# The context in two transfers, and a new order of W_audio's and W_text's first work on TensorE

## The chip, the cores and the metric

One core of a Trainium2 chip runs the kernel. The time is device microseconds (us) of one execution; lower is better. The engines are TensorE (PE; its weight loads are listed apart as PEld), VectorE (DVE), ScalarE (ACT), GpSimd (POOL) and SyncE (SP, which here only issues transfers; SPq and ACTq are the queues of issues). Each engine works through its own instructions in order and waits on semaphores for the others.

## What is computed

A cross attention: 4 batches of 2048 rows of x (512 wide) attend to 4 batches of 77 context rows (384 wide).

```python
text_p = einsum('bld,dh->blh', x, W_text) + b_text          # 512 -> 512
audio_p = einsum('bsd,dh->bsh', ctx, W_audio) + b_audio     # 384 -> 512
Q = layer_norm(text_p, g1, beta1)
K = layer_norm(audio_p, g2, beta2)
alpha = softmax(einsum('blh,bsh->bls', Q, K) / sqrt(512))
hyper = einsum('bls,bsh->blh', alpha, audio_p)
hyper = einsum('blh,hk->blk', hyper, W_out) + b_out
out = layer_norm(hyper + x, g_out, beta_out)
```

## The kernel before

The kernel does not form Q. In a setup it turns the weights and the context into per-batch matrices, among them the Gram matrix of the centred W_text, from which the variance of a row of `text_p` follows, and the score weights W_text x K. The steady part then takes x in 32 steps of 256 rows: TensorE transposes x and multiplies it with these matrices, ScalarE and VectorE split each operand in a high and a low part, and the rest of the layer norms and the softmax follows. The steady part is the same after the change. The change lies in the first third of the setup.

Every engine's program is written out by hand, and its order is the order of the work. The names that matter:

- SyncE (L315 to L325) issues the loads: the context `cx` (77 partitions, 4 batches, 384 columns; `ctx_loaded`), then blocks of 128 rows of W_audio (`load_audio(0..2)`) and of W_text (`load_text(0..3)`), then W_out. The next thing it issues are the loads of x, after `linear(1)` on VectorE.
- TensorE begins with ten warm-up products (`keep_busy`, L1190). Then come twelve transposes of the context (L1214, four for each block k of 128 columns, a batch each), which ScalarE copies to `cxT` (L576, in order of k). `audio_product(j, k)` (L1202) multiplies block j of W_audio with block j of the context into bank k; each takes two passes of 308 columns. It waits for `cxT_ready` of j + 1. The last one for bank k, j = 2, releases `audio(k)` on ScalarE (L564, two copies: `vT` and `vT_hi`).
- The vectors (g1, b_audio and others) are transposed (L1219) and copied by VectorE (L850, `vec_ready`).
- VectorE centres W_text: `centre_even(k)` itself (L834 to L836), `centre_odd` (L841) with a row sum that ScalarE makes (`text_sum`, L558, behind the three copies to `cxT` in ScalarE's order). `text_transposes(j)` (L1195) waits for block j to be centred; when the fourth block is through, ScalarE copies the high part (`wtT_hi`, L593, behind `audio(0)` in its order) and VectorE makes the low part (`text_lo(k)`, L871).
- VectorE also makes `gram_kept` and `gram_left` (L859 to L863), from which GpSimd makes `root` (L430); `root_cols` (L878) follows after the fourth `text_lo`. It sums and centres `b_text` (L866, L867, L879), and makes the low part of the projected context (`keys_lo(k)`, L892).
- TensorE's `gram(k)` (L1239) waits in its first round for `text_lo(h)`. After `gram(0)`, the transposes of the root (L1250) and the first half of `gram(1)` comes the mean over the projected context (L1260). It waits for all four `keys_lo` (`vT_lo_ready`). Behind it, in TensorE's order: the rest of `gram`, the values (L1284) and the key scales (L1294), with which VectorE goes on (L955).

The order on TensorE around the change, before:

```python
pe.wait_ge(ctx_loaded, 16)
for k in range(KA):
    ...                                  # four transposes, cxT_psum
for k in range(KH):
    audio_product(0, k)
...                                      # the transpose of the vectors
for k in range(KH):
    audio_product(1, k)
audio_product(2, 0)
...
text_transposes(0); text_transposes(1); text_transposes(2); text_transposes(3)
audio_product(2, 1); audio_product(2, 2); audio_product(2, 3)
```

Of the kernel before, what the change touches and what calls it, by code (L numbers as in the profile page):

```python
# [25 lines left out]
ALU = mybir.AluOpType  # L26
ACT = mybir.ActivationFunctionType
AX_X = mybir.AxisListType.X

P = 128  # L30
# [3 lines left out]
def cross_attention(nc, x, ctx, w_text, b_text, w_audio, b_audio, w_out, b_out,  # L34
                    g1, beta1, g2, beta2, g_out, beta_out, out):
    B, L, D = x.shape
    _, S, DA = ctx.shape
    H = w_text.shape[1]
    KD, KA, KH = D // P, DA // P, H // P
# [24 lines left out]
    with ExitStack() as stack:  # L64
        f32 = lambda ap: ap.bitcast(F32)

        def sb(name, shape, dt=F32):
            return stack.enter_context(nc.sbuf_tensor(name, shape, dt))

        def sem(name):  # L70
            return stack.enter_context(nc.semaphore(name))
# [14 lines left out]
        wtT_hi, wtT_lo = wtT[:, 0], wtT[:, 1]  # L86
# [37 lines left out]
        bt_rows = sb("bt_rows", [P, H])  # L124
# [12 lines left out]
        sums = sb("sums", [P, 16])  # L137
# [24 lines left out]
        cx = values[:, 0:B * DA].rearrange("p (b d) -> p b d", b=B)[0:S]  # L162
# [24 lines left out]
        wt_loaded = [sem(f"wt_loaded{k}") for k in range(KD)]  # L187
        wa_loaded = [sem(f"wa_loaded{j}") for j in range(KA)]
        wo_loaded = [sem(f"wo_loaded{n}") for n in range(2)]
        ctx_loaded, vec_loaded = sem("ctx_loaded"), sem("vec_loaded")  # L190
        bt_loaded, bo_loaded = sem("bt_loaded"), sem("bo_loaded")
        gs_loaded, t_copied = sem("gs_loaded"), sem("t_copied")
        mean_r_ready = sem("mean_r_ready")
# [6 lines left out]
        wtT_hi_ready, wtT_lo_ready, lin_ready = sem("wtT_hi_ready"), sem("wtT_lo_ready"), sem("lin_ready")  # L200
# [22 lines left out]
        W_BANK = (psT[:], B_BANK[0], psD[:], psO[:])  # L223
# [81 lines left out]
        def _(sp):  # L305
# [3 lines left out]
            def load_text(k):  # L309
                sp.dma_start(wt[:, k, :], wt_rows[:, k, :]).then_inc(wt_loaded[k], 16)  # L310

            def load_audio(j):
                sp.dma_start(wa[:, j, :], wa_rows[:, j, :]).then_inc(wa_loaded[j], 16)

            sp.dma_start(cx, ctx.rearrange("b s d -> s b d")).then_inc(ctx_loaded, 16)  # L315
            load_audio(0)
            load_text(0)
            load_audio(1)
            load_text(1)
            load_text(2)  # L320
            load_audio(2)
            load_text(3)
            wo_rows = w_out.rearrange("(k p) h -> p k h", p=P)
            for n in range(2):
                sp.dma_start(wo[:, 2 * n:2 * n + 2, :], wo_rows[:, 2 * n:2 * n + 2, :]).then_inc(wo_loaded[n], 16)  # L325
# [496 lines left out]
        def _(dve):  # L822
            own = [0]

            def link(ins):

                own[0] += 1
                ins.then_inc(dve_own, 1)
                dve.wait_ge(dve_own, own[0])
# [13 lines left out]
            def gram_dot(k):  # L843
                dve.wait_ge(wc_ready, k + 1)
                nc.vector.tensor_tensor_reduce(out=waste_dve[:, k, 0:H], in0=wt[:, k, :], in1=wt[:, k, :], scale=1.0, scalar=0.0,
                                               op0=ALU.mult, op1=ALU.add, accum_out=gram_diag[:, k:k + 1]).then_inc(gram_dot_ready, 1)
# [7 lines left out]
            gram_dot(2)  # L854
            gram_dot(3)

            dve.wait_ge(gram_sq_ready, 2)
            dve.wait_ge(gram_dot_ready, 2)
            nc.vector.tensor_scalar(gram_kept[:], gram_diag[:], KEPT, None, ALU.mult).then_inc(kept_ready, 1)  # L859
# [2 lines left out]
            dve.wait_ge(left_ready, 1)  # L862
            nc.vector.tensor_scalar(gram_left[:], gram_left[:], 1e-30, None, ALU.max).then_inc(left_ready, 1)  # L863

            dve.wait_ge(bt_loaded, 16)
            link(nc.vector.reduce_sum(sums[:, 4:5], bt_rows[:], axis=AX_X))  # L866
            link(nc.vector.tensor_scalar(sums[:, 5:6], sums[:, 4:5], -1.0 / H, None, ALU.mult))  # L867

            def text_lo(k):
                dve.wait_ge(wtT_hi_ready, k + 1)  # L870
                nc.vector.tensor_tensor(wtT_lo[:, k, :], W_BANK[k], f32(wtT_hi[:, k, :]), ALU.subtract).then_inc(wtT_lo_ready, 1)  # L871

            text_lo(0)
            text_lo(1)
            text_lo(2)
            text_lo(3)
            dve.wait_ge(root_ready, 1)
            nc.vector.tensor_copy(root_cols[:], root[:]).then_inc(root_cols_ready, 1)  # L878
            nc.vector.tensor_scalar(bt_rows[:], bt_rows[:], sums[:, 5:6], None, ALU.add).then_inc(bc_ready, 1)  # L879

            def t_lo(k):
# [300 lines left out]
        def _(pe):  # L1182
# [9 lines left out]
            def text_transposes(j):  # L1192
                pe.wait_ge(wc_ready, j + 1)
                for k in range(KH):
                    last = nc.tensor.transpose(W_BANK[k][:, j * P:(j + 1) * P], wt[:, j, k * P:(k + 1) * P], ident[:])  # L1195
                    if j == KD - 1:
                        last.then_inc(wtT_psum, 1)

            def audio_product(j, k):
                pe.wait_ge(wa_loaded[j], 16)  # L1200
                pe.wait_ge(cxT_ready, j + 1)
                last = nc.tensor.matmul(V_BANK[k][:, 0:BS], wa[:, j, k * P:(k + 1) * P], cxT[:, j, :],  # L1202
                                        start=(j == 0), stop=(j == KA - 1))
                if j == KA - 1:
                    last.then_inc(vT_psum, 1)
# [2 lines left out]
            pe.wait_ge(ones_ready, 1)  # L1208
            keep_busy(10, psE)
            pe.wait_ge(ident_ready, 1)  # L1210
            pe.wait_ge(ctx_loaded, 16)
            for k in range(KA):
                for b in range(B):
                    last = nc.tensor.transpose(CTX_BANK[k][:, b * S:(b + 1) * S], cx[:, b, k * P:(k + 1) * P], ident[0:S, 0:S])  # L1214
                last.then_inc(cxT_psum, 1)
            for k in range(KH):
                audio_product(0, k)
            pe.wait_ge(vec_loaded, 16 * len(VECS))
            nc.tensor.transpose(VEC_BANK[:, 0:len(VECS) * KH], vec_rows[:], ident[0:len(VECS) * KH, 0:len(VECS) * KH]).then_inc(vec_psum, 1)  # L1219
            for k in range(KH):  # L1220
                audio_product(1, k)
            audio_product(2, 0)
            pe.wait_ge(vec_ready, 1)
            pe.wait_ge(cxT_ready, KA)
            text_transposes(0)
            text_transposes(1)
            text_transposes(2)
            text_transposes(3)
            audio_product(2, 1)
# [284 lines left out]
```

## Time and profile before

| what | us |
|---|---|
| median of 3 runs (lowest, highest) | 264.65 (264.42, 264.94) |
| the profiled execution | 264.86 |
| its span, first to last instruction | 263.1 |
| TensorE busy in it | 251.4 (96%) |
| VectorE busy | 231.6 (88%) |
| ScalarE busy | 217.5 (83%) |
| GpSimd busy | 203.2 (77%) |

A share of busy time is an average over stages. The rows below give a start, a duration and what was waited for; with them one can follow which engine is last at a given point. Matmuls are pipelined, so the listed duration of one is longer than the time until the next can start; starts of successive instructions tell the pace.

### The profile page before, as it was taken

What the parts mean: (1) busy time and instruction counts of PE and PEld (TensorE: products, weight loads), DVE (VectorE), ACT (ScalarE), POOL (GpSimd) and SP (SyncE); (2) the same over time, 40 slices, a digit from 0 to 9 for tenths busy, and PEclk for the clock granted to TensorE, in tenths of its full rate; (3) what the DMA queues carried; (4) which work ended last, traced back from release to release, by engine and by line L of the source; (5) the groups of instructions that cost most, each with busy time, mean ns of one, the idle gap of its engine ahead of it and who ended that gap; (6) DMA issues with size and microseconds to landing.
All of it is one profiled execution on the core that took longest, in us unless ns stands there. A gap on an engine that the chain in (4) does not pass through costs nothing.

```text
span 263.1 us, 6007 instructions
## 1 busy us (share of the span) xinstructions
PE 251.4 (96%) x1671; PEld 234.4 (89%) x1671; DVE 231.6 (88%) x712; ACT 217.5 (83%) x575; POOL 203.2 (77%) x213
## 2 busy tenths in 40 slices
PE   8999999999999999999999999999999999999860
PEld 8789888989999999999999999999999999998730
DVE  0797799789999999999999999999999999999884
ACT  3696385246999999999999999999999999999970
POOL 8139450021399999999999999999999999999694
PEclk9999999999999999999999999999999999999997
DMA  6901769544345444454554445455444454553036
GB/s 196 357 2 40 183 216 392 166 120 151 105 148 163 171 166 165 168 167 166 167 166 159 159 161 159 161 159 159 161 159 166 168 166 172 168 173 148 0 161 239
DMA packets 19489, 43.26 MB, mean 164 GB/s; under 512 B 2082, under 2 KB 2414, under 8 KB 19466
## 3 DMA queue, kind: packets, MB, share of 16 engines
q1 hardware_dynamic: 18842, 41.96, 47.2%
q10 hardware_dynamic: 624, 1.06, 1.6%
q14 instruction: 17, 0.14, 0.2%
q8 instruction: 6, 0.10, 0.2%
HBM read 21.19 MB, written 16.78 MB: 144 GB/s over the span
## 4 chain that ended last, share of the span: by engine, by line
PE 79%; SPq 6%; DVE 5%; POOL 4%; issue 2%; ACT 1%; DMA 1%; POOLq 0%; DVEq 0%; ACTq 0%
PE psY L1407 26%; PE psY L1391 12%; PE psT L1320 10%; PE psO L1427 10%; SPq L344 6%; PE psY L1386 4%; PE psE L1370 3%; PE psE L1371 2%; PE psY L1202 2%; PE psE L1190 2%; POOL zs L525 1%; DMA xs<-in_x_dram 1%; PE psT L1284 1%; PE psT L1239 1%; POOL rstd L500 1%
## 5 line engine op out<-in xcount | busy, mean ns | idle before, releaser
L1407 PE MATMUL psY<-proj,x_hi 128*128 128x336 f32 x512 | 102.5, 322 | 0.0
L1407 PEld LDWEIGHTS psY<-proj,x_hi 128*128 128x128 f32 x512 | 84.1, 189 | 5.5
L475 POOL TENSOR_TENSOR zs<-zs,gain 128x512 f32<-128x512 f32 x55 | 71.2, 1294 | 3.8 <-ACT zs L696 3.8
L481 POOL TENSOR_TENSOR zs<-zs,shift 128x512 f32<-128x512 f32 x54 | 68.5, 1291 | 0.0
L487 POOL TENSOR_TENSOR rstd<-stat_eps,neg_half 128x4 f32<-128x4 f32 x30 | 30.5, 1017 | 33.1 <-DVE stat_eps L1044 33.1
L1391 PE MATMUL psY<-proj,x_lo 128*128 128x336 f32 (+1 forms) x256 | 54.2, 313 | 0.0
L1032 DVE CUSTOM_DVE_ANT_0 waste_dve<-psY,xs,sums 128x515 bf16<-128x515 f32 x64 | 48.4, 756 | 2.3
L1052 DVE SCALAR_TENSOR_TENSOR hid<-psO,inv_sum,xs 128x512 f32<-128x512 f32 x60 | 44.8, 747 | 3.2 <-PE psO L1427 0.6
L696 ACT ACTIVATE zs<-hid,shift,rstd 128x512 f32<-128x512 f32 x58 | 47.1, 813 | 0.0
L654 ACT ACTIVATE x_hi<-psT 128x512 fp32r<-128x512 f32 x64 | 38.1, 596 | 8.8 <-PE psT L1320 6.9
L685 ACT ACTIVATE waste_act<-hid,xs 128x512 bf16<-128x512 f32 x60 | 43.1, 718 | 1.4 <-DVE hid L1052 1.3
L907 DVE TENSOR_TENSOR x_lo<-psT,x_hi 128x512 fp32r<-128x512 f32 x64 | 43.7, 683 | 0.4 <-ACT x_hi L654 0.2
L1391 PEld LDWEIGHTS psY<-proj,x_lo 128*128 128x128 f32 x256 | 40.3, 189 | 0.0
L1320 PE MATMUL psT<-ident,xs 128*128 128x128 f32 x256 | 39.7, 278 | 0.1
L1320 PEld LDWEIGHTS psT<-ident,xs 128*128 128x128 f32 x256 | 28.1, 141 | 1.9 <-DMA xs<-in_x_dram 0.3
L1427 PE MATMUL psO<-wo_hi,parts_t 128*128 128x512 f32 x60 | 26.9, 448 | 0.2 <-ACT parts_t L727 0.2
L1386 PE MATMUL psY<-proj,x_lo 128*128 128x128 f32 (+1 forms) x128 | 26.8, 251 | 0.0
L713 ACT ACTIVATE psD<-logits,neg_max 128x77 f32<-128x77 f32 x62 | 19.8, 319 | 7.7 <-DVE neg_max L1067 7.7
L1427 PE MATMUL psO<-wo_lo,parts_t 103*128 103x512 f32 x60 | 23.9, 398 | 0.0
L1386 PEld LDWEIGHTS psY<-proj,x_lo 128*128 128x128 f32 x128 | 23.1, 188 | 0.0
L727 ACT ACTIVATE parts_t<-psE 128x512 fp32r<-128x512 f32 x31 | 18.6, 599 | 2.7 <-PE psE L1371 1.8
L1370 PE MATMUL psE<-ident,parts 128*128 128x128 f32 x62 | 15.9, 284 | 1.3 <-DVE parts L1077 1.3
(272 smaller groups left out, 430.8 us busy)
## 6 DMA issues: line engine op xcount, KB each, us to landing
xs<-in_x_dram SPq DMA_DIRECT2D x64, 256.0 KB, 3.0
out_dram<-zs SPq DMA_DIRECT2D x29, 512.0 KB, 3.9
proj<-proj SPq DMA_DIRECT2D x4, 768.0 KB, 6.9
out_dram<-zs SPq DMA_DIRECT2D x6, 256.0 KB, 2.2
xs<-in_L_xattn_W_text_dram SPq DMA_DIRECT2D x4, 256.0 KB, 5.4
xs<-in_L_xattn_W_out_dram SPq DMA_DIRECT2D x2, 512.0 KB, 7.4
wa<-in_L_xattn_W_audio_dram SPq DMA_DIRECT2D x3, 256.0 KB, 5.1
zs<-in_ctx_dram SPq DMA_DIRECT2D x1, 462.0 KB
```

The source lines that it names most:

```text
L475: nc.gpsimd.tensor_tensor(zs[:, q, t, :], zs[:, q, t, :], gain[:], ALU.mult).then_inc(zg_ready, 1)
L481: nc.gpsimd.tensor_tensor(zs[:, q, t, :], zs[:, q, t, :], shift[:], ALU.add).then_inc(out_ready, 1)
L685: nc.scalar.activation(waste_act[:, t, :], hid[:, (b - 3) % 2, t, :], ACT.Square, bias=sc[:, q, t, NX:NX + 1], accum_out=stat[:, (b + 1) % ...
L696: nc.scalar.activation(zs[:, q, t, :], hid[:, q % 2, t, :], ACT.Identity, bias=shift2[:, q, t:t + 1], scale=rstd[:, q, T + t:T + t + 1]).t ...
L907: nc.vector.tensor_tensor(x_lo[:, b % 2, t, :], psT[:], f32(x_hi[:, b % 2, t, :]), ALU.subtract).then_inc(x_lo_ready, 1)
L1032: nc.vector.tensor_tensor_reduce(out=waste_dve[:, t, 0:QUAD_W], in0=psY[:, t, QUAD_AT:QUAD_AT + QUAD_W], in1=xs_rows[:, q, t, X_AT - 1:X_A ...
L1052: nc.vector.scalar_tensor_tensor(hid[:, (b - 3) % 2, t, :], psO[:], inv_sum[:, q, t:t + 1], xs[:, q, t, :], ALU.mult, ALU.add).then_inc(hi ...
L1320: last = nc.tensor.transpose(psT[:, k * P:(k + 1) * P], xs[:, b, t, k * P:(k + 1) * P], ident[:])
L1386: return nc.tensor.matmul(psY[:, t, B_AT + SW + k * P:512], x_lo[:, par, t, k * P:(k + 1) * P], proj[:, q, k, SW + k * P:HALF], start=Fals ...
L1391: return nc.tensor.matmul(psY[:, t, 512 + skip:512 + HALF], x_lo[:, par, t, k * P:(k + 1) * P], proj[:, q, k, HALF + skip:ROW_W], start=Fa ...
L1407: nc.tensor.matmul(psY[:, t, to:to + HALF], x_hi[:, par, t, k * P:(k + 1) * P], proj[:, q, k, right * HALF:(right + 1) * HALF], start=(k = ...
L1427: last = nc.tensor.matmul(psO[:], parts_t[0:rows, (b - lag) % 2, t, n, :], v[0:rows, q, :], start=(n == 0), stop=(n == 1))
```

## The change

It touches four places. (1) The context comes in two transfers: its first 128 columns, then W_audio's first block, then the context's other 256 columns; each has a semaphore of its own. W_text's fourth block is loaded before W_audio's third. (2) On TensorE the four products of W_audio's first block stand right behind the first four context transposes, and the other eight transposes behind those products. (3) The first product of W_audio's third block moves from before W_text's transposes to between the second and the third of its four blocks. (4) On VectorE `text_lo(0)` moves ahead of `gram_kept` and `gram_left`, and the sum over `b_text` moves from before the `text_lo` to behind `root_cols`.

```diff
+            ctx_rows = ctx.rearrange("b s d -> s b d")
+            sp.dma_start(cx[:, :, 0:P], ctx_rows[:, :, 0:P]).then_inc(ctx_loaded[0], 16)
             load_audio(0)
+            sp.dma_start(cx[:, :, P:DA], ctx_rows[:, :, P:DA]).then_inc(ctx_loaded[1], 16)
             load_text(0)
             load_audio(1)
             load_text(1)
             load_text(2)
+            load_text(3)
             load_audio(2)
-            load_text(3)
...
+            text_lo(0)
             dve.wait_ge(gram_sq_ready, 2)
             dve.wait_ge(gram_dot_ready, 2)
...
-            dve.wait_ge(bt_loaded, 16)
-            link(nc.vector.reduce_sum(sums[:, 4:5], bt_rows[:], axis=AX_X))
-            link(nc.vector.tensor_scalar(sums[:, 5:6], sums[:, 4:5], -1.0 / H, None, ALU.mult))
...
-            text_lo(0)
             text_lo(1)
             text_lo(2)
             text_lo(3)
             dve.wait_ge(root_ready, 1)
             nc.vector.tensor_copy(root_cols[:], root[:]).then_inc(root_cols_ready, 1)
+            dve.wait_ge(bt_loaded, 16)
+            link(nc.vector.reduce_sum(sums[:, 4:5], bt_rows[:], axis=AX_X))
+            link(nc.vector.tensor_scalar(sums[:, 5:6], sums[:, 4:5], -1.0 / H, None, ALU.mult))
             nc.vector.tensor_scalar(bt_rows[:], bt_rows[:], sums[:, 5:6], None, ALU.add).then_inc(bc_ready, 1)
...
-            pe.wait_ge(ctx_loaded, 16)
-            for k in range(KA):
+
+            def context_transposes(k):
+                pe.wait_ge(ctx_loaded[min(k, 1)], 16)
                 for b in range(B):
                     last = nc.tensor.transpose(CTX_BANK[k][:, b * S:(b + 1) * S], cx[:, b, k * P:(k + 1) * P], ident[0:S, 0:S])
                 last.then_inc(cxT_psum, 1)
+
+            context_transposes(0)
             for k in range(KH):
                 audio_product(0, k)
+            context_transposes(1)
+            context_transposes(2)
...
             for k in range(KH):
                 audio_product(1, k)
-            audio_product(2, 0)
             pe.wait_ge(vec_ready, 1)
             pe.wait_ge(cxT_ready, KA)
             text_transposes(0)
             text_transposes(1)
+            audio_product(2, 0)
             text_transposes(2)
             text_transposes(3)
             audio_product(2, 1)
```

## Rows read from the trace of the kernel before

**Rows 1.** Busy time by stretch: from:to, length, busy (instructions) PE PEld DVE ACT POOL, PEclk, DMA share, GB/s.
```profile
0.00:30.20 30.20, 29.15 (x165) 25.52 (x166) 19.02 (x54) 17.14 (x41) 17.03 (x43) 1.00 0.46 147
...
63.50:240.00 176.50, 176.43 (x1221) 169.77 (x1222) 165.65 (x529) 166.65 (x446) 162.88 (x136) 1.00 0.49 162
```

**Rows 2.** The chain that ended last, in order of time: start, us, what.
```profile
19.80 1.14 PE psY L1260 x8
...
43.59 0.93 SPq L344
```

**Rows 3.** Timeline, weight loads of gram and mean: start, us, what [idle before, releaser].
```profile
15.22 2.65 PEld L1239 LDWEIGHTS psT<-wtT 128*128 128x128 f32 x12 [0.17 <-DVE wtT L871]
...
19.47 0.64 PEld L1260 LDWEIGHTS psY<-vT_hi,kg_hi 128*128 128x128 f32 x4
```

**Rows 4.** Timeline of VectorE, 9 to 20 us.
```profile
9.48 0.18 DVE L850 COPY vec_cols<-psO 128x24 f32<-128x24 f32 x1 [1.34 <-PE psO L1219]
9.58 0.48 DVE L841 TENSOR_SCALAR xs<-xs,sums 128x512 f32<-128x512 f32 x1
...
13.09 0.17 DVE L859 TENSOR_SCALAR gram_kept<-gram_diag 128x4 fp32r<-128x4 f32 x1
...
13.57 0.68 DVE L866 TENSOR_REDUCE sums<-bt_rows 128x1 f32<-128x512 f32 x1
...
14.47 0.69 DVE L871 TENSOR_TENSOR wtT<-psT,wtT 128x512 fp32r<-128x512 f32 x1
...
16.87 0.16 DVE L878 CAST root_cols<-root 128x4 fp32r<-128x4 f32 x1
...
17.34 1.43 DVE L892 SCALAR_TENSOR_TENSOR vT_lo<-psY,vec_cols,vT_hi 128x308 fp32r<-128x308 f32 x3
18.67 0.53 DVE L892 SCALAR_TENSOR_TENSOR vT_lo<-psE,vec_cols,vT_hi 128x308 fp32r<-128x308 f32 x1
```

**Rows 5.** Timeline of TensorE and the context's issue, 0 to 15 us.
```profile
0.80 0.43 SPq L315 DMA_DIRECT2D zs<-in_ctx_dram  x1
...
1.05 4.34 PEld L1190 LDWEIGHTS psE<-hid 128*128 128x128 f32 x20 [1.05 <-POOL hid L399]
...
5.58 0.55 PEld L1214 LDWEIGHTS psT<-ident,zs 77*128 77x128 f32 x4 [0.19 <-issue]
...
6.53 0.39 PEld L1214 LDWEIGHTS psD<-ident,zs 77*128 77x128 f32 x4
...
8.59 0.68 PE L1202 MATMUL psE<-cxT,wa 128*128 128x308 f32 x2
...
9.20 0.14 PEld L1219 LDWEIGHTS psO<-ident,vec_rows 24*128 24x128 f32 x1 [0.42 <-issue]
...
11.03 0.68 PE L1202 MATMUL psE<-cxT,wa 128*128 128x308 f32 x2
...
13.81 1.20 PE L1202 MATMUL psY<-cxT,wa 128*128 128x308 f32 x4
```

**Rows 6.** Timeline of ScalarE, 6 to 14 us.
```profile
6.39 0.43 ACT L576 ACTIVATE cxT<-psT 128x308 f32<-128x308 f32 x1 [1.44 <-PE psT L1214]
...
8.06 0.63 ACT L558 ACTIVATE waste_act<-xs 128x512 bf16<-128x512 f32 x1 [0.47 <-DMA xs<-in_L_xattn_W_text_dram]
...
12.33 0.52 ACT L564 ACTIVATE vT<-psY,vec_cols 128x308 f32<-128x308 f32 x1 [0.95 <-PE psY L1202]
12.74 0.51 ACT L564 ACTIVATE vT_hi<-psY,vec_cols 128x308 fp32r<-128x308 f32 x1
...
13.69 0.60 ACT L593 ACTIVATE wtT<-psT 128x512 fp32r<-128x512 f32 x1 [0.43 <-PE psT L1195]
```

**Rows 7.** One line's instructions: ns min/median/max, first and last start.
```profile
L887 DVE CUSTOM_DVE_ANT_0 waste_dve<-xs,bt_rows x4: 685/820/1514, 19.1 to 35.4; 128x512 bf16<-128x512 f32 x4
```

**Rows 8.** Timeline of GpSimd: the root and the low parts of W_out.
```profile
13.75 1.04 POOL L430 TENSOR_TENSOR root<-gram_left,half 128x4 f32<-128x4 f32 x1 [6.48 <-DVE gram_left L863]
...
18.79 5.51 POOL L434 TENSOR_TENSOR wo_lo<-xs,wo_hi 128x512 fp32r<-128x512 f32 x4 [4.00 <-ACT wo_hi L572]
```

More of the change, by code:

```diff
@@ L189, in cross_attention @@
         wo_loaded = [sem(f"wo_loaded{n}") for n in range(2)]
-        ctx_loaded, vec_loaded = sem("ctx_loaded"), sem("vec_loaded")
+        ctx_loaded, vec_loaded = [sem(f"ctx_loaded{n}") for n in range(2)], sem("vec_loaded")
         bt_loaded, bo_loaded = sem("bt_loaded"), sem("bo_loaded")
@@ L313, in load_audio @@
                 sp.dma_start(wa[:, j, :], wa_rows[:, j, :]).then_inc(wa_loaded[j], 16)
-            sp.dma_start(cx, ctx.rearrange("b s d -> s b d")).then_inc(ctx_loaded, 16)
+            ctx_rows = ctx.rearrange("b s d -> s b d")
+            sp.dma_start(cx[:, :, 0:P], ctx_rows[:, :, 0:P]).then_inc(ctx_loaded[0], 16)
             load_audio(0)
+            sp.dma_start(cx[:, :, P:DA], ctx_rows[:, :, P:DA]).then_inc(ctx_loaded[1], 16)
             load_text(0)
@@ L855, in _, with text_lo @@
             gram_dot(3)
+            def text_lo(k):
+                dve.wait_ge(wtT_hi_ready, k + 1)
+                nc.vector.tensor_tensor(wtT_lo[:, k, :], W_BANK[k], f32(wtT_hi[:, k, :]), ALU.subtract).then_inc(wtT_lo_ready, 1)
+            text_lo(0)
             dve.wait_ge(gram_sq_ready, 2)
@@ L863, in _ @@
             nc.vector.tensor_scalar(gram_left[:], gram_left[:], 1e-30, None, ALU.max).then_inc(left_ready, 1)
-            dve.wait_ge(bt_loaded, 16)
-            link(nc.vector.reduce_sum(sums[:, 4:5], bt_rows[:], axis=AX_X))
-            link(nc.vector.tensor_scalar(sums[:, 5:6], sums[:, 4:5], -1.0 / H, None, ALU.mult))
-            def text_lo(k):
-                dve.wait_ge(wtT_hi_ready, k + 1)
-                nc.vector.tensor_tensor(wtT_lo[:, k, :], W_BANK[k], f32(wtT_hi[:, k, :]), ALU.subtract).then_inc(wtT_lo_ready, 1)
-            text_lo(0)
             text_lo(1)
```

## The prediction

> **What bounds the kernel now.** I read the busy time by stage first, then the chain of waits, then the timelines of the first 21 us. From 63.5 us to 240 us TensorE is busy 176.43 of 176.50 us [rows 1]: nothing that the change touches lies there, so all it can do is to let this stretch begin earlier or later. What sets that beginning is read from the chain [rows 2]: TensorE without a break up to the key scales, VectorE from there through value_lo(0), SyncE's queue from 43.59 with the placing of the values, a load of x, and then TensorE's steady work. There is no slack in this chain: each piece is released by the one before. The mean product (L1260, on the chain from 19.80) stands in it, so a delay of that product goes through to the end one for one, and so would a gain. I therefore cost the change at one place: when can L1260 start?
>
> Before, two things come together there. TensorE's order brings its first weight load at 19.47 [rows 3]; VectorE ends the last keys_lo, for which L1260 waits, at 18.67 + 0.53 = 19.20 [rows 4]. VectorE is only 0.27 ahead. Both paths must be followed.
>
> **Part by part, TensorE.** The warm-up products end at 1.05 + 4.34 = 5.39 on the load side, and the first context transposes load at 5.58, 0.19 later, without a releaser in the profile [rows 5]. I take this as the context's landing; the smaller front transfer then removes it. The end of the warm-up stays, so the gain is 0 to 0.19; I take 0.17, the other end being that the gap is only the cost of the two waits. The extra transfer costs SyncE one more issue, 0.43 [rows 5]. What it is moved past (W_text, W_audio, W_out) shares one saturated stretch of transfers with unchanged bytes, and SyncE then has nothing to issue until the loads of x, late in the setup: 0 for the path. Were a block of W_text half a microsecond late, VectorE's 1.34 us of idle time before L850 would hide it [rows 4].
>
> Before, the eight transposes of the context's second and third part ran while ScalarE copied the first; the first product began at about 8.59 - 3 x 0.52 = 7.03 [rows 5]. After, nothing stands between. ScalarE starts its copy 0.17 earlier than 6.39 and takes 0.43 [rows 6], so 6.65; 0.06 until TensorE loads (as 14.47 + 0.69 to 15.22 [rows 3, 4]), some 0.2 for that load: 6.9. The four products take 2.08, to 8.98. Then come the eight transposes, 0.10 each at the pace of the third four (0.39 for 4 [rows 5]): 9.76. The transpose of the vectors took 0.36 (9.11 to 11.03 - 3 x 0.52 = 9.47), part of it behind a load idle of 0.42 [rows 5], which is gone by then: 0.2 to 0.36, I take 0.2. So W_audio's second block starts at 9.98 instead of 9.47: **0.5 late**, since the products didn't replace the transposes but went ahead of them, into a gap. From there on the order changes, not the sum: 4 + 1 products of 0.52 and 16 transposes of 0.11 (12.07 to 13.81 [rows 5]).
>
> **ScalarE and VectorE up to text_lo(0).** ScalarE works in order. Its copies of the context's second and third part now wait for transposes that end near 10.05, so text_sum (8.06 before [rows 6]) begins at about 10.5; VectorE's centring of W_text's second block waits for it until about 11.2 instead of 9.58. From that to gram_kept VectorE took 13.09 - 9.58 = 3.5 [rows 4]: free at 14.7. That is hidden, by 0.4, because text_lo(0) can't start before that anyway: the product that releases audio(0) on ScalarE now lies between the transposes of W_text's second and third block, ends at 9.98 + 2.08 + 0.88 + 0.52 = 13.46, and ScalarE answers 0.26 later (12.07 to 12.33). Its two copies come 0.41 apart [rows 6], so wtT_hi(0) starts at 13.46 + 0.26 + 0.82 = 14.53 instead of 13.69. The transposes themselves would allow 14.2. text_lo(0) waits for its end and starts at about **15.2** instead of 14.47.
>
> **VectorE from there to L1260.** This is the term that decides. Before, VectorE used its time ahead of text_lo(0) for gram_kept to gram_left (13.57 - 13.09 = 0.48) and for the sum over b_text (14.47 - 13.57 = 0.90) [rows 4]. After, both stand behind text_lo(0), in front of keys_lo, and VectorE sits idle ahead of it. In order: text_lo(0) 0.61, gram_kept to gram_left 0.48, three text_lo 1.79, root_cols 0.07, the sum 0.90, the centring of b_text 0.40, keys_lo 19.20 - 17.34 = 1.86 [rows 4]: 15.18 + 6.11 = 21.29 instead of 19.20. The root on GpSimd (1.04 [rows 8]) has the 1.8 us from gram_left to root_cols, so it is hidden by 0.8. TensorE on its own would be there about 1.1 late (gram starts 0.7 later with text_lo(0), then waits 0.4 for text_lo(1)), so VectorE is the later one. L1260 loads at 21.35; it has no gram left to hide the load, so its products start at about 21.54 instead of 19.80: **+1.75 us**.
>
> What is behind the waiting product on TensorE: the rest of gram, the values, the key scales, all without a break of its own. linear(0) on VectorE takes 1.51 beside GpSimd and 0.69 without it [rows 7]; it ends near 22.7, just when the mean is there.
>
> **Sum.** The profiled execution took 264.86 us, 263.1 of them the span; 264.86 + 1.75 = 266.6. It lies 0.21 above the median of the runs, so I put the median after at **266.4**.
>
> **The rivals.**
> *GpSimd meets the moved work.* GpSimd's first wo_lo starts at 18.79 [rows 8]; ScalarE's delay of 0.8 moves it to about 19.6, and the centring of b_text now ends at 19.4. If GpSimd comes first, that centring or a neighbour is lengthened as linear(0) is, 1.51 - 0.69 = 0.83: 267.2. The margin of 0.2 speaks against it. The Trainium skill (SBUF — State Buffer, Who interferes with whom) says that VectorE's tensor_scalar can need the port pair that it shares with GpSimd, and that whoever issues second is blocked for the whole instruction; by that rule this centring is open to it and the sum over b_text, a reduction, is not, and the 1.51 of linear(0) agrees.
> *TensorE alone is the bound.* If VectorE runs tighter than its rows, TensorE's own +1.1 remains: 265.7.
> *TensorE's clock.* After the warm-up there would be four transposes and a gap of some 0.6 before the first products. The granted clock reads 1.00 (2.4 GHz) for the first 30 us [rows 1], yet four loads of the context take 0.55 first and 0.39 later [rows 5], and the warm-up's 20 loads took 4.34, 0.22 for 128 columns. At that pace a pass over 308 columns takes 0.52 instead of 0.26, and the first four products, two passes each, 2.1 longer; with the 1.75, and a little for transposes, 268.8. Against it: the pace rose before, within the transposes. The Trainium skill (TensorE: Matmul & The Clock Gate, Part 4) says that transposes do not count as busy for the clock as products do; by that rule the rise could come later here, but the rise among transposes shows that it need not.
> *Nothing to measure.* The delay is taken up between 21 and 63 us: 264.65. The unbroken chain speaks against it.
> *Faster.* The transposes of parts two and three fall into waits that the profile hides, and VectorE reaches keys_lo in time. Then 0.13 at the first product, 0.16 at the vectors and about 0.25 at gram (the load wait of 0.17 and text_lo(0) no longer behind the sum over b_text) come off: 264.1. It decides at text_lo(0): 6.1 us of VectorE work stand between it and L1260, so it would have to start near 13.5, which the end of the warm-up excludes by more than 1 us.
>
> **How the numbers follow.** Forecast (VectorE late for L1260, +1.2 to +2.3) 0.66; GpSimd 0.08; TensorE alone 0.08; clock 0.04; nothing 0.07; faster 0.07. The first four are slower, 0.86. The range 265.3 to 267.4 takes in the forecast, with a late text_lo(0) at either end of its bounds, TensorE alone and GpSimd; 0.18 is left out. Differences under 0.2%, 0.53 us, can't be told from none here.
>
> **What the profile after would show.** A gap of about 0.5 us on TensorE between the first four context transposes and the first product; vec_cols near 10.0; VectorE idle before text_lo(0), which starts near 15.2; keys_lo ending near 21.3, and TensorE idle 0.4 to 0.7 before L1260; the key scales and everything behind them about 1.75 later. The forecast is wrong if keys_lo ends before TensorE is through with gram's first rows, or if L1260's delay is not found again at 63.6.

## The result, and the profile after

The changed kernel takes **266.97 us** (median of 6 executions, 266.49 to 268.57); the kernel before, on the same chip beside it, 264.93 us (264.42 to 265.31, 6 executions). The ratio is 1.0077, with a 95% interval of 1.0048 to 1.0106: slower by about 2 us, with a spread that is more than twice that of before. A second set of 6 executions gave 266.66 us (265.90 to 268.55) beside 264.81, ratio 1.0079 [1.0052, 1.0107]. Over the whole study the kernel before took 264.25 to 265.54 us in 43 executions of 44, and 267.43 in one. Two slow runs, 279.08 us of the kernel before and 270.48 us of transposes_in_front (below), are left out of all medians, ratios and counts.

This spread matters for reading the trace, so two profiles of the same kernel stand side by side here: its longest execution, 268.57 us, and its shortest, 265.90 us. No profile was taken of an execution near the median. Some lines of the kernel moved by a few numbers: context transposes are L1216, products L1203, gram L1245, the mean product L1266, text_lo L861, keys_lo L893, the key scales L1300.

TensorE in the longest execution (timeline: start, us, engine, line, operation, tile, count, [idle before, releaser]):

```profile
1.05 4.64 PE L1191 MATMUL psE<-hid 128*128 128x128 f32 x20 [1.05 <-POOL hid L401]
5.48 0.72 PE L1216 MATMUL psT<-ident,zs 77*128 77x77 f32 x4
6.81 3.42 PE L1203 MATMUL psY<-cxT,wa 128*128 128x308 f32 x6 [0.61 <-ACT cxT L578]
10.02 0.83 PE L1203 MATMUL psE<-cxT,wa 128*128 128x308 f32 x2
...
11.73 1.79 PE L1203 MATMUL psY<-cxT,wa 128*128 128x308 f32 x6 [0.18 <-ACT cxT L578]
...
23.24 0.81 PE L1266 MATMUL psY<-vT_hi,kg_hi 128*128 128x308 f32 x4 [0.63 <-DVE vT_lo L893]
```

The same lines in the shortest:

```profile
1.05 3.85 PE L1191 MATMUL psE<-hid 128*128 128x128 f32 x20 [1.05 <-POOL hid L401]
4.74 0.43 PE L1216 MATMUL psT<-ident,zs 77*128 77x77 f32 x4
5.78 1.79 PE L1203 MATMUL psY<-cxT,wa 128*128 128x308 f32 x6 [0.61 <-ACT cxT L578]
...
8.97 1.79 PE L1203 MATMUL psY<-cxT,wa 128*128 128x308 f32 x6 [0.17 <-ACT cxT L578]
...
20.48 0.81 PE L1266 MATMUL psY<-vT_hi,kg_hi 128*128 128x308 f32 x4 [0.60 <-DVE vT_lo L893]
```

The same places in the kernel before, with the first VectorE instruction behind the key scales (L955):

```profile
6.96 1.79 PE L1202 MATMUL psY<-cxT,wa 128*128 128x308 f32 x6
...
9.37 1.82 PE L1202 MATMUL psY<-cxT,wa 128*128 128x308 f32 x6
...
19.64 0.73 PE L1260 MATMUL psY<-vT_hi,kg_hi 128*128 128x308 f32 x4
...
30.17 1.87 DVE L955 SCALAR_TENSOR_TENSOR hid<-hid,vec_cols,psY 128x308 f32<-128x308 f32 x4 [0.87 <-PE psY L1294]
```

Two things are the same in both executions of the changed kernel: TensorE idles 0.61 us between the first context transposes and the first product, and the mean product waits 0.6 us for VectorE's keys_lo. Before, the second of these waits wasn't there [rows 2, 3]. What differs is TensorE's pace, from the warm-up on. The warm-up products take 4.64 us in the one and 3.85 in the other, the first transposes 0.72 and 0.43, and the first six passes over W_audio 3.42 and 1.79, about 0.51 a pass against 0.26. In the longest execution the pace was thus still low before the idle time of 0.61; in the shortest it had risen before it. From the second block's start to the mean product it is 23.24 - 11.73 = 11.51 us in the longest and 20.48 - 8.97 = 11.51 in the shortest. So the two executions differ only ahead of that block.

VectorE in the longest execution, the lines that answer to [rows 4], and the first instruction behind the key scales:

```profile
11.59 0.18 DVE L852 COPY vec_cols<-psO 128x24 f32<-128x24 f32 x1 [1.91 <-PE psO L1225]
12.65 0.49 DVE L843 TENSOR_SCALAR xs<-xs,sums 128x512 f32<-128x512 f32 x1 [0.88 <-ACT waste_act L560]
...
16.98 0.69 DVE L861 TENSOR_TENSOR wtT<-psT,wtT 128x512 fp32r<-128x512 f32 x1 [0.92 <-ACT wtT L595]
17.58 0.16 DVE L866 TENSOR_SCALAR gram_kept<-gram_diag 128x4 fp32r<-128x4 f32 x1
...
19.92 0.68 DVE L878 TENSOR_REDUCE sums<-bt_rows 128x1 f32<-128x512 f32 x1
...
22.57 0.53 DVE L893 SCALAR_TENSOR_TENSOR vT_lo<-psE,vec_cols,vT_hi 128x308 fp32r<-128x308 f32 x1
...
33.86 1.43 DVE L956 SCALAR_TENSOR_TENSOR hid<-hid,vec_cols,psY 128x308 f32<-128x308 f32 x3 [0.87 <-PE psY L1300]
```

VectorE idles 0.88 us for ScalarE's sums over W_text (L560) and 0.92 us for ScalarE's wtT_hi(0) ahead of text_lo(0). Then gram_kept and the sum over b_text, which stood in such idle time before, follow it, and keys_lo ends at 23.10 instead of 19.20 [rows 4]; 2.36 us of that is the later start of W_audio's second block (11.73 against 9.37).

Where does the time go behind that? Nowhere else. The busy time of the longest execution by stretch, as in [rows 1] (from:to, length, busy (instructions) of PE, PEld, DVE, ACT, POOL, PEclk, DMA share, GB/s):

```profile
0.00:30.20 30.20, 27.63 (x146) 23.16 (x147) 16.75 (x44) 16.91 (x41) 14.83 (x40) 1.00 0.39 129
63.50:240.00 176.50, 176.50 (x1223) 169.58 (x1223) 165.62 (x530) 165.64 (x442) 159.30 (x133) 1.00 0.48 160
```

All of the loss lies in the first 30 us, where TensorE is busy 1.52 us less than before. The first VectorE instruction behind the key scales starts at 33.86 here and at 30.17 before: 3.69 late, and this execution took 268.57 - 264.86 = 3.71 us longer. In the shortest execution it starts at 31.10, 0.93 late, for 1.04 us. What is lost at the mean product stays lost.

### The profile page after: what moved, and what is told of

Same layout as the page of the kernel before. It is cut to its first block, busy times and chain, and to the rows that moved or that the text cites. A ratio compares the mean times of both kernels' runs of the same rounds, so it can differ in the third digit from the quotient of the medians.

```text
span 266.8 us, 6007 instructions
## 1 busy us (share of the span) xinstructions
PE 253.6 (95%) x1671; PEld 235.2 (88%) x1671; DVE 231.8 (87%) x712; ACT 217.4 (81%) x575; POOL 203.3 (76%) x213
## 3 DMA queue, kind: packets, MB, share of 16 engines
q10 hardware_dynamic: 624, 1.06, 1.4%
## 4 chain that ended last, share of the span: by engine, by line
PE 84%; POOL 4%; DVE 4%; ACT 3%; issue 2%; POOLq 0%; ACTq 0%; DVEq 0%
PE psY L1413 27%; PE psY L1397 12%; PE psT L1326 11%; PE psO L1433 10%; PE psY L1392 4%; PE psE L1376 3%; PE psE L1377 2%; PE psY L1203 2%; PE psY L1290 2%; PE psY L1336 2%; PE psE L1191 2%; POOL zs L527 1%; PE psT L1290 1%; POOL rstd L502 1%; POOL zs L523 1%
```

## The experiments

The table reads two starts from every kernel's profiled execution: that of W_audio's second block (here a1) and that of the mean product. "Behind key scales" is how much later than in before (30.17) the first VectorE instruction behind them starts; the last two columns are what that execution took beyond before's 264.86, and the median over all executions of the kernel with its ratio to before. All differences are of numbers in the traces.

| kernel | a1 | mean | a1 to mean | behind key scales | this execution | median, ratio [95%] |
|---|---|---|---|---|---|---|
| before | 9.37 | 19.64 | 10.27 | 0 | 0 | 264.81 to 264.93 |
| short_warmup | 10.97 | 21.25 | 10.28 | +1.61 | +1.77 | 267.62, 1.0106 [1.0090, 1.0121] |
| sum_ahead | 10.35 | 20.59 | 10.24 | +0.95 | +0.91 | 265.94, 1.0053 [1.0032, 1.0074] |
| products_first | 10.20 | 21.12 | 10.92 | +1.49 | +1.83 | 266.15, 1.0054 [1.0037, 1.0070] |
| vector_order_back | 9.77 | 20.70 | 10.93 | +1.07 | +0.87 | 265.87, 1.0046 [1.0019, 1.0073] |
| fill_and_vector_back | 10.00 | 20.92 | 10.92 | +1.28 | +1.24 | 266.10, 1.0043 [1.0029, 1.0057] |
| third_block_back | 9.65 | 20.82 | 11.17 | +1.23 | +1.20 | 266.07, 1.0051 [1.0037, 1.0066] |
| vector_order_alone | 9.37 | 20.58 | 11.21 | +0.99 | +0.95 | 266.13, 1.0054 [1.0039, 1.0068] |
| after, longest | 11.73 | 23.24 | 11.51 | +3.69 | +3.71 | 266.97, 1.0077 [1.0048, 1.0106] |
| after, shortest | 8.97 | 20.48 | 11.51 | +0.93 | +1.04 | 266.66, 1.0079 [1.0052, 1.0107] |
| gap_filled | 9.25 | 20.76 | 11.51 | +1.20 | +1.55 | 266.23, 1.0056 [1.0044, 1.0069] |
| one_transfer | 10.08 | 21.59 | 11.51 | +2.04 | +2.10 | 266.96, 1.0079 [1.0065, 1.0093] |
| transposes_in_front | 12.11 | 23.64 | 11.53 | +4.05 | +4.38 | 267.70, 1.0097 [1.0069, 1.0124] |

The fourth column falls into four values, whatever the start: 10.24 to 10.28, 10.92 or 10.93, 11.17 to 11.21, and 11.51 to 11.53. It depends only on the order in which the engines work, and it is the part of the loss that every execution pays. The second column is the part that differs from one execution to the next. Most medians in the last column lie within about 1 us of each other, with intervals that overlap, so the argument below rests on the traces and not on these medians. The experiments take the two columns apart. The kernel of each is an edit of the changed kernel or of the one before, as said.

**VectorE's order put back.** The changed kernel with text_lo(0) behind the sum over b_text again.

```
-            text_lo(0)
             dve.wait_ge(gram_sq_ready, 2)
...
+            dve.wait_ge(bt_loaded, 16)
+            link(nc.vector.reduce_sum(sums[:, 4:5], bt_rows[:], axis=AX_X))
...
+            text_lo(0)
             text_lo(1)
```

> The changed kernel with VectorE's order of before (gram_kept, gram_left and the sum over b_text ahead of text_lo(0)). In the changed kernel VectorE is through with gram_dot only about 0.5 us before text_lo(0) can start, so the work put back there (0.48 + 0.90) makes text_lo(0) itself some 0.9 later, and takes 1.4 off behind it. Theory 'both orders together': L1260's wait shortens by only about 0.4, the fastest executions come to 266.0 to 266.3 against 266.5 of the changed kernel, and the spread between executions stays (up to 2 us). Rival 'VectorE's order is the loss': 265.0 to 265.4.

Measured: 265.87 us, 1.1 or 0.8 less than the two sets of the changed kernel. The expectations spoke of the fastest execution: it took 265.31 us, in the range of the rival, while the median lies between the two. The trace tells more than these times. VectorE and TensorE in it:

```profile
10.70 0.48 DVE L843 TENSOR_SCALAR xs<-xs,sums 128x512 f32<-128x512 f32 x1 [0.88 <-ACT waste_act L560]
...
15.60 0.69 DVE L873 TENSOR_TENSOR wtT<-psT,wtT 128x512 fp32r<-128x512 f32 x1
...
16.34 3.01 PE L1246 MATMUL psT<-wtT 128*128 128x512 f32 x12 [0.44 <-DVE wtT L873]
...
20.70 0.73 PE L1267 MATMUL psY<-vT_hi,kg_hi 128*128 128x308 f32 x4
```

Behind the 0.88 VectorE has no idle time left, and text_lo(0) begins when VectorE gets there, not when ScalarE is ready. The mean product waits for nothing: TensorE is the later one now, 20.70 against 19.64. It comes late because a1 is 0.40 later and because gram waits 0.44 us for this text_lo(0). So VectorE's order decides in the changed kernel: from a1 to the mean 10.93 us with its old order, 11.51 with the new. Right under it lies a second limit, worth 1.06 us in this profile.

**VectorE's order alone**, in the kernel before: the sum over b_text and the gram_kept lines behind text_lo(0), as the change has them.

```
+            text_lo(0)
             dve.wait_ge(gram_sq_ready, 2)
...
-            text_lo(0)
             text_lo(1)
...
+            link(nc.vector.reduce_sum(sums[:, 4:5], bt_rows[:], axis=AX_X))
```

> The kernel before with VectorE's new order alone. VectorE would stand idle from 13.0 until wtT_hi(0) ends at 14.29, text_lo(0) at about 14.35, keys_lo's end 6.1 later at 20.5, L1260's products at 20.7 instead of 19.8. Theory: 0.8 to 1.0 slower, 265.6 to 265.9, with the narrow spread of before (0.9). Rival 'VectorE's order costs nothing where TensorE is on time': 264.7. Rival 'VectorE's order is the whole loss': 266.4 and more.

```profile
14.32 0.69 DVE L859 TENSOR_TENSOR wtT<-psT,wtT 128x512 fp32r<-128x512 f32 x1 [1.34 <-ACT wtT L593]
...
20.58 0.81 PE L1259 MATMUL psY<-vT_hi,kg_hi 128*128 128x308 f32 x4 [0.60 <-DVE vT_lo L891]
```

Measured: 266.13 us, a little above what was expected. text_lo(0) starts only 0.15 earlier than in [rows 4], after an idle time of 1.34 us, and the mean product then waits for keys_lo. From a1 to the mean it is 11.21 instead of 10.27: +0.94 us with nothing else changed.

**The first products ahead of the other transposes, alone**, in the kernel before, with its single transfer, its order on VectorE and its third block:

```
+            context_transposes(0)
             for k in range(KH):
                 audio_product(0, k)
+            context_transposes(1)
+            context_transposes(2)
```

> The kernel before with one thing of the change alone: four W_audio products right behind the first four context transposes, and the other eight transposes behind them; context in one transfer, VectorE's order and the third audio block as before. Theory (ScalarE's second copy to cxT then stands later, and text_sum behind it): second block of W_audio at 10.0 to 10.1, centre_odd(0) at 11.0 after a wait for text_sum, text_lo(0) at about 15.9, the means at about 21.0: 266.0 to 266.2, with single executions up to 268. Rival (only TensorE's lost half microsecond counts): 265.3 to 265.5.

```profile
9.63 0.43 ACT L576 ACTIVATE cxT<-psY 128x308 f32<-128x308 f32 x1 [2.76 <-PE psY L1215]
...
11.12 0.49 DVE L841 TENSOR_SCALAR xs<-xs,sums 128x512 f32<-128x512 f32 x1 [0.88 <-ACT waste_act L558]
...
16.02 0.69 DVE L871 TENSOR_TENSOR wtT<-psT,wtT 128x512 fp32r<-128x512 f32 x1
...
21.12 0.73 PE L1265 MATMUL psY<-vT_hi,kg_hi 128*128 128x308 f32 x4
```

Measured: 266.15 us, as the theory had it; the rival, that only TensorE's lost half microsecond counts, falls. ScalarE waits 2.76 us for transposes that now come late, its sums over W_text stand behind that copy, and VectorE's centring waits for them at 11.12 (9.58 in [rows 4]). Of the 1.48 us at the mean, 0.83 is a1 (10.20 against 9.37) and 0.65 is this chain through ScalarE. The expected tail up to 268 wasn't seen in its six executions (266.05 to 266.81). The 10.92 is that of vector_order_back too: there the second limit is this chain.

**The sums put ahead on ScalarE**, on top of that kernel:

```
             for k in range(KA):
...
+                if k == 0:
+                    load_row(bt_rows, b_text, bt_loaded)
+                    text_sum(0, 1)
```

> The same kernel as products_first, with ScalarE's load of b_text and its text_sum of the first two chunks moved between its first and its second copy to cxT. Theory: centre_odd(0) back at about 10.1, text_lo(0) at about 15.1, the means at about 20.2: 265.3 to 265.5, single slow executions remaining. Rival (ScalarE's order is not on the path): the same time as products_first, within 0.2 us.

```profile
5.99 0.56 PE L1216 MATMUL psT<-ident,zs 77*128 77x77 f32 x4 [0.30 <-DMA zs<-in_ctx_dram]
...
8.24 0.63 ACT L558 ACTIVATE waste_act<-xs 128x512 bf16<-128x512 f32 x1 [1.23 <-DMA xs<-in_L_xattn_W_text_dram]
...
10.31 0.48 DVE L842 TENSOR_SCALAR xs<-xs,sums 128x512 f32<-128x512 f32 x1
...
20.59 0.73 PE L1266 MATMUL psY<-vT_hi,kg_hi 128*128 128x308 f32 x4
```

The centring no longer waits, and a1 to the mean is 10.24 again, as before the change: the 0.65 was ScalarE's order. The time is 265.94 us, above the 265.3 to 265.5 expected, and only 0.2 below products_first: a1 was 0.98 late instead of the 0.5 assumed, in part because the context came later in this execution (the first transposes at 5.99, after a wait for it, against 5.61 before), and two of the eight executions took 267.28 and 267.52. The mechanism is shown in the trace; by the medians alone the gain could not be told from nothing.

**The third block of W_audio put back** ahead of W_text's transposes, in the changed kernel:

```
                 audio_product(1, k)
+            audio_product(2, 0)
...
             text_transposes(1)
-            audio_product(2, 0)
             text_transposes(2)
```

> The changed kernel with the first product of W_audio's third block ahead of W_text's transposes again. audio(0) on ScalarE then ends before the transposes do, and wtT_hi(0) starts with TensorE (0.3 earlier relative to W_audio's second block). Theory: text_lo(0) 0.2 to 0.3 earlier, bounded by VectorE's gram_dot; fastest executions 266.2 to 266.4, the spread up to 2 us stays. Rival 'this move was the cause of text_lo(0) being late': 265.6 or less for the fastest. Rival 'it is free': 266.5.

```profile
14.56 0.69 DVE L861 TENSOR_TENSOR wtT<-psT,wtT 128x512 fp32r<-128x512 f32 x1 [0.58 <-ACT wtT L595]
...
20.82 0.80 PE L1266 MATMUL psY<-vT_hi,kg_hi 128*128 128x308 f32 x4 [0.61 <-DVE vT_lo L893]
```

Measured: 266.07 us (265.81 to 266.57): the fastest is under the expected 266.2, above the rival's 265.6, and the expected spread of 2 us wasn't seen in the five executions. text_lo(0) starts 14.56 - 9.65 = 4.91 us behind a1, against 16.98 - 11.73 = 5.25 in the changed kernel: the split of the transposes costs 0.34 us, because the product that releases ScalarE's copies stands one half of the transposes later. With it gone, a1 to the mean is 11.17, the same as VectorE's order alone gives (11.21): the chain through ScalarE lies under VectorE's order and adds nothing to it. The two are not summed; the later one counts. The 1.24 us that the change adds between a1 and the mean is then that of VectorE's order (0.94 alone) and of the third block (0.34), 1.28 together.

**One transfer for the context**, all else as in the changed kernel:

```
-            sp.dma_start(cx[:, :, 0:P], ctx_rows[:, :, 0:P]).then_inc(ctx_loaded[0], 16)
+            sp.dma_start(cx, ctx.rearrange("b s d -> s b d")).then_inc(ctx_loaded, 16)
             load_audio(0)
-            sp.dma_start(cx[:, :, P:DA], ctx_rows[:, :, P:DA]).then_inc(ctx_loaded[1], 16)
```

> The changed kernel with the context in one transfer again; every engine's order stays. In the runs so far the two transfers bring 319 more packets, and W_text's first block is read at 8.0 to 8.4 instead of 6.7 to 6.8. Theory 'hidden': the late loads only use up VectorE's idle time before the vectors (1.3 us before, 0 to 0.3 in the runs with two transfers), so with one transfer W_text is read at 6.7 again but text_lo(0) stays with TensorE and ScalarE, and the first transposes wait for the whole context (0.15 later): fastest executions 266.5 to 266.8, spread up to 2 us as in the changed kernel. Rival 'the late loads are a part of the loss': 265.7 to 266.1 for the fastest.

```profile
6.89 1.79 PE L1201 MATMUL psY<-cxT,wa 128*128 128x308 f32 x6 [0.61 <-ACT cxT L576]
...
21.59 0.81 PE L1264 MATMUL psY<-vT_hi,kg_hi 128*128 128x308 f32 x4 [0.60 <-DVE vT_lo L891]
```

Measured: 266.96 us (266.54 to 267.28), the same as with two transfers; the fastest is where 'hidden' had it, and the expected spread wasn't seen in five executions. In an execution whose warm-up runs at the slow pace the first transposes start at 5.54 with one transfer and at 5.48 with two: the warm-up products last that long anyway, and the front transfer's earlier landing is hidden behind them. It isn't where the pace rises in the warm-up: in the shortest execution the first transposes start at 4.74.

**The transposes all in front**, with the context still in two transfers, to close the gap on TensorE:

```
-            context_transposes(0)
+            for k in range(KA):
+                context_transposes(k)
             for k in range(KH):
                 audio_product(0, k)
-            context_transposes(1)
-            context_transposes(2)
```

> The changed kernel with all twelve context transposes ahead of W_audio's products again; the two transfers, the later product of W_audio's third block and VectorE's new order stay. No gap on TensorE and ScalarE's copies to cxT are early again. Theory: W_audio's second block starts at about 9.3 to 9.4 again, text_lo(0) near 14.5, L1260's products near 20.8: 265.6 to 265.9, and with the gap the spread goes: no execution over 266.3. Rival 'the spread has nothing to do with the gap': executions up to 2 us above the fastest remain. Rival 'TensorE's order is free': 266.5.

```profile
4.80 0.43 PE L1216 MATMUL psT<-ident,zs 77*128 77x77 f32 x4
7.51 0.77 PE L1216 MATMUL psY<-ident,zs 77*128 77x77 f32 x4 [2.27 <-DMA zs<-in_ctx_dram]
...
8.59 2.90 PE L1203 MATMUL psY<-cxT,wa 128*128 128x308 f32 x6
```

Measured: 267.70 us (266.13 to 269.24). The expectation failed because the second transfer lands only at 7.5, so the edit made a gap of 2.27 us instead of closing one. It was of use in another way: the pace was already high for the first transposes (0.43 for four), and behind the gap it is low again (0.77). In this trace the granted clock is on record in the same stretch (columns as in [rows 1]):

```profile
4.00:5.00 1.00, 1.00 (x11) 1.00 (x11) 0.00 (x0) 0.94 (x4) 0.85 (x4) 1.00 0.83 264
...
8.00:9.00 1.00, 1.00 (x8) 1.00 (x7) 0.93 (x3) 0.59 (x2) 0.00 (x0) 0.50 1.00 381
```

It falls from 1.00 to 0.50, that is from 2.4 to 1.2 GHz, and the passes start 0.51 us apart, as in the longest execution of the changed kernel. There the column reads 1.00 for the same passes: in these first microseconds it can't be relied on, the duration of a pass can.

**The gap filled** with two warm-up products, in the changed kernel:

```
             context_transposes(0)
+            keep_busy(2, psE)
             for k in range(KH):
```

> The changed kernel with two more warm-up products between the first four context transposes and W_audio's first products, in the gap of 0.8 us (two of them take 0.9 at the pace of the warm-up). Theory 'the gap makes TensorE's pace rise later in some executions': all executions within 0.9 of each other, 266.5 to 267.2, the first four products at 0.26 a pass. Rival 'the pace rises at its own time, gap or not': the spread of 2 us stays, with executions over 267.5.

```profile
5.02 0.43 PE L1216 MATMUL psT<-ident,zs 77*128 77x77 f32 x4
5.29 0.65 PE L1191 MATMUL psE<-hid 128*128 128x128 f32 x4
6.06 1.79 PE L1203 MATMUL psY<-cxT,wa 128*128 128x308 f32 x6
```

Measured: 266.23 us, mostly under the expected 266.5 to 267.2. The six executions lie within 0.67 us (265.88 to 266.55), where those of the changed kernel spread over 2.1 and 2.65. The profile can't tell what the filling did: the pace had risen before it, as the first transposes show.

**The gap filled and VectorE's order back** together, the edits of both kernels:

> The changed kernel with VectorE's order of before and with two warm-up products in the gap. Theory: both gains hold side by side: no execution over 266.4 (the spread of 3 us without the fill goes), the median at 265.3 to 265.7, TensorE not waiting for keys_lo. What then stays against the kernel before (264.9) is the gap of TensorE itself, 0.5 to 0.8. Rival 'the fill costs as much as it saves in a normal execution': median 265.9 to 266.2.

```profile
5.48 0.72 PE L1217 MATMUL psT<-ident,zs 77*128 77x77 f32 x4
5.99 0.88 PE L1192 MATMUL psE<-hid 128*128 128x128 f32 x4
6.81 1.79 PE L1204 MATMUL psY<-cxT,wa 128*128 128x308 f32 x6
```

Measured: 266.10 us, again within 0.67, against 265.87 for vector_order_back, whose twelve executions reach 268.39. The median is where the rival had it, but its reason is not in the trace. The first product starts 0.61 us behind the end of the first transposes (5.48 + 0.72 to 6.81), as it does without the filling, so the filling costs nothing here. a1 is 0.23 later than in vector_order_back because these transposes, which stand ahead of the filling, took 0.72 us instead of 0.49. The difference of the medians is also within the intervals.

Nor is it shown that the filling takes the long executions away. Six of the 48 executions of the kernels that keep the 0.61 us of idle time lie above 267.3 us, none of the 11 of the two filled kernels, and one of 44 of the kernel before, which has no such idle time. At a rate of six in 48, eleven executions without a long one are to be expected about one time in four.

**A shorter warm-up** in the kernel before (four rounds instead of ten), to make a gap there, with no other edit:

```
-            keep_busy(10, psE)
+            keep_busy(4, psE)
```

> The kernel before with four warm-up products instead of ten, and nothing else changed: TensorE then stands idle from about 3 us until the context has landed, about 2.4 us, and the first context transpose shows when it lands (5.4 to 5.6 if the 0.19 before it was that wait; earlier if it was not). Theory 'an idle gap early makes TensorE's pace rise later in some executions': the first products run at 0.5 a pass instead of 0.26 in several executions; the fastest executions stay at 264.4 to 265.0, the median goes to 265.5 or more, single ones to 267 to 268. Rival 'the pace rises at its own time, gap or not': all as before, 264.3 to 265.5.

```profile
5.50 0.75 PE L1214 MATMUL psT<-ident,zs 77*128 77x77 f32 x4 [2.37 <-DMA zs<-in_ctx_dram]
...
7.07 3.29 PE L1202 MATMUL psY<-cxT,wa 128*128 128x308 f32 x6
```

Measured: 267.62 us (266.63 to 267.71). The median rose as expected, but all four executions are long: the fastest was expected at 264.4 to 265.0. In its profile the first products are slow, and a1 is 1.60 later while a1 to the mean stays 10.28. The edit makes a gap of 2.37 us, but it also takes away six of the ten warm-up products, and the pace was low before the gap already (eight warm-up passes in 2.07 us). Whether the gap or the shorter warm-up keeps it low is not told apart. The trace also shows when the whole context is there in this execution: about 5.5.

**The changed kernel again**, unaltered, for a profile of another execution:

> The changed kernel once more, unaltered, to see a profile of an ordinary execution beside the slowest one. Theory (TensorE's pace rises late in some executions only): executions mostly at 266.4 to 266.8, one or two up to 268.6. If the profiled one is near 266.5, its first six W_audio products take .26 us a pass (some 1.8 us) and the means' products start at 21.4 to 21.6; if it is above 267.5, they take .51 a pass (3.4 us) and the means start after 22.5. Rival (the slow first products are part of every execution of the change): 3.4 us for the six in a profile near 266.5 too.

Its profile is the shortest execution shown above, 265.90 us, so neither of the two cases that were expected, near 266.5 or above 267.5, was seen. The slow products are not part of every execution: here the pace had risen by the first transposes (0.43 us for four at 4.74), a microsecond ahead of the first product.

## Why the prediction was right

Forecast 266.4 (265.3 to 267.4), measured 266.97 and 266.66. The mechanism was right: VectorE is late for the mean product, by nearly the amount forecast, and the delay goes through. That the medians themselves lie so near is in part luck, since the pace moves single executions by more than the error of the forecast: the two that were profiled are 3.69 and 0.93 us late behind the key scales, where the forecast had 1.75. By its own steps:

- **Where the loss would be read**: at the mean product, passed on one for one. It holds in every run of the table: the shift behind the key scales and the execution's own time agree within 0.35 us.
- **From a1 to the mean**: the forecast had 10.33 before (9.47 to 19.80) and 11.56 after (9.98 to 21.54), +1.23. Measured +1.24 (10.27 to 11.51). The parts are right too: 5.2 from a1 to text_lo(0) (measured 5.25), then 6.11 of VectorE's work to the end of keys_lo (measured 22.57 + 0.53 - 16.98 = 6.12). VectorE's idle time ahead of text_lo(0) and TensorE's 0.4 to 0.7 ahead of the mean are there, 0.92 (the forecast's margin was 0.4) and 0.63. That VectorE's late wait for text_sum is hidden holds as well (third_block_back).
- **a1 itself**: forecast +0.51. In the execution that is nearest to the forecast's assumptions (one_transfer: the first product at 6.89, forecast 6.9) it is +0.71. The forecast overlooked that a1 needs the context's second copy on ScalarE, a wait of 0.17 on TensorE. The 0.17 gained by the front transfer is too much for executions with a slow warm-up: the traces show 0.13 (5.61 to 5.48), or 0.06 against one_transfer.
- **The mean product itself**: without gram's work to hide its loads it holds TensorE for 24.47 - 23.24 = 1.23 us instead of 20.78 - 19.64 = 1.14. The 0.09 wasn't in the sum. Summed anew, 0.71 + 1.24 + 0.09 = 2.04, which is what one_transfer shows behind the key scales. In absolute times the forecast is nearer: the mean at 21.54, where one_transfer has 21.59, and a1 at 9.98 against 10.08. It took its starts of before too late, 9.47 and 19.80, where the timeline has 9.37 and 19.64.
- **The clock**: put down as a rival for all executions, with a chance of 0.04 and 268.8 us. It is true of some. The price of 268.8 came near, 268.57 measured and 268.55 once more, but its part for the slow passes was too high: 2.1, where the longest execution needs 1.73 more from the first product to a1 (4.92 against 3.19), since the pace rose during the last passes. The step that failed is to treat the pace as one state of the kernel; it differs between executions, and 3 of the 12 of the changed kernel lie above the range, and where it rises early it saves time, as in the shortest execution.
- **The front transfer, 0 for the path**: held in time. But "unchanged bytes" was too simple. The queue that carries the loads handled 319 packets more, and the first read of W_text starts on VectorE at 8.28 (7.64 in the shortest execution), against 6.56 with one transfer. The 1.34 us of cover that the forecast named [rows 4] is used up in the shortest execution.

The queue in the page of the changed kernel, and of the one with a single transfer (packets, MB, share of 16 engines):

```profile
q1 hardware_dynamic: 19161, 41.96, 46.4%
```

```profile
q1 hardware_dynamic: 18842, 41.96, 46.1%
```

- **GpSimd**: its wo_lo starts at 21.45, behind the centring of b_text (20.82 + 0.49), by 0.14, near the margin forecast. So the rival wasn't put to the test. linear(0) is slow, 1.52, as forecast; but its price is not fixed, as the forecast had it: in products_first it takes 0.75 and in vector_order_back 1.10 while GpSimd works on wo_lo.
- **TensorE alone**: its 1.1 us is in the changed kernel's own trace. There TensorE would have been ready at 23.24 - 0.63 = 22.61, which is 10.88 behind a1 and 0.61 more than before; with the 0.5 forecast for a1 that is 1.1. It lies under the bound that decided. That vector_order_back took 265.87, near the 265.7 of this rival, is in part luck: there text_lo(0) is late through ScalarE's sums, a chain that the forecast had as hidden.

No kernel of this study beats the one before. What the change wants, an earlier start of the first product, it gets: in its own two profiles this is at 6.81 and 5.78, against 6.96 before. But even the execution with 5.78 is 1.04 us slower. With the old order on VectorE and of the third block, and ScalarE's sums put ahead, a1 to the mean is that of before again (sum_ahead, 10.24). What remains is a1, late because eight transposes and a wait now stand behind the first products instead of in a gap. From the first product to a1 it is 9.37 - 6.96 = 2.41 us before, and 3.19 in every profile with the new order and fast passes: 0.78 more.

## What to carry to other kernels

An order in which every engine is rarely idle has its steps in each other's gaps. Before moving a step to the front, ask which engine's in-order work stands behind it: here moving eight transposes delayed ScalarE's copies, behind them its sums, and behind these VectorE. Work that fills an engine's wait (the sum over b_text) costs its full length once it stands behind the thing waited for. And a pause in TensorE's start can cost more than the pause: behind 2.27 us of it passes took 0.51 us that take 0.26 at the high pace. For a pause of 0.61 us this is not shown. Compare the spread of executions, not only their median.

## What the hardware showed beside

- After a pause TensorE's pace comes up later in some executions and not in others. A pause of 0.61 us behind the first transposes was followed by passes of 0.51 us in one profiled execution of the changed kernel and of 0.26 us in the other, but the pace before the pause differed in the same way; in one_transfer and products_first it was low before the pause and high behind it. After pauses of 2.27 and 2.37 us the passes were slow in both profiles taken, the twelve transposes of short_warmup among them (0.75, 0.72, 0.72 for four). Only in the first of the two was the pace high before. The Trainium skill (TensorE: Matmul & The Clock Gate, Part 4) says that transposes do not count as busy for the clock as products do; these twelve are in line with it but don't show it, since the products behind them stayed slow as well; in the kernel before the pace rose among the transposes (0.74, 0.67 and 0.43 us for four). What sets the moment in one execution stays open. The kernel before, without the pause, had one long execution of 44; third_block_back, one_transfer and products_first, which keep it, had none above 267.3 in 16.
- A transfer in two column pieces of the same rows moved the same bytes in 319 more packets. Its second piece, issued third, landed at 7.5 us in transposes_in_front, while the whole in one transfer was there at 5.5 in short_warmup and at 6.0 in sum_ahead.
